# A block of attention, state space scan and routed LoRA on one core: the router's small steps split between VectorE and GpSimd, and the order of all queues written anew

## What is computed

```python
h = layernorm(x) * (1 + ca) + sa
xn = ln(h)
attn_out = causal_attention(xn, 16 heads of 16) @ o_w + o_b
x_c = silu(causal_conv4(xn @ in_proj_w[:, :512]) + conv_b);  z = xn @ in_proj_w[:, 512:]
dt = softplus(x_dbc[..., :16] @ dt_w + dt_b);  B, C = x_dbc[..., 16:32], x_dbc[..., 32:48]   # x_dbc = x_c @ x_proj_w
for t: state = exp(dt * A) * state + (x_c * dt) * B;  y[t] = sum_n C * state     # 512 channels, 16 states each
r = h + alpha * attn_out + (1 - alpha) * (((y + x_c * D) * silu(z)) @ ssm_out_w)
r = r + gelu(ln(r) @ ffn_w1 + b1) @ ffn_w2 + b2
x = x + ga * r
g = layernorm(x) * (1 + cb) + sb
logits = g @ router_w + router_b                    # 8 experts
w = softmax(where(logits < second_largest, -1e9, logits))
x = x + gb * (g @ base_w + base_b + 2.0 * sum_e w[e] * (g @ A_e) @ B_e)
```

## Time and profile before

| | us |
|---|---|
| median of 3 runs | 5759.91 (5759.66 to 5764.49) |
| the profiled execution, its own time | 5763.4 |
| its span from first to last instruction | 5761.6 |
| one turn of the loop (the softplus sum starts at 108.6 and, 31 turns on, at 5479.2) | 173.25 |

### The profile page before, as it was taken

The page is one execution under the profiler, slowest core; times in us unless marked ns, Lnnn a source line. Parts: engine busy times, 40 slices in busy tenths (PEclk is TensorE's granted clock), DMA queues, the critical chain, the costliest instruction groups (busy, mean ns, idle before and its releaser), DMA issues.

```text
span 5761.6 us, 94560 instructions
## 1 busy us (share of the span) xinstructions
PE 5214.0 (90%) x32280; PEld 3490.0 (61%) x32280; DVE 5161.4 (90%) x7776; ACT 4082.5 (71%) x6407; POOL 4217.8 (73%) x2545
## 2 busy tenths in 40 slices
PE   4799998999999999999999999999999999999986
PEld 2466665666666566666566656666656666666664
DVE  4999999999999999999999999999999999999983
ACT  3777777767777777777777777777777777777763
POOL 3777777777777777777777777777777777777762
PEclk7899999999999999999999999999999999999998
DMA  4444445444444444444444445444454445554441
GB/s 127 145 146 140 146 143 147 146 148 133 151 136 153 143 145 140 145 142 154 142 143 138 142 150 151 143 138 143 143 155 147 142 139 146 143 151 145 140 128 39
DMA packets 521455, 812.22 MB, mean 141 GB/s; under 512 B 80432, under 2 KB 227288, under 8 KB 520976
## 3 DMA queue, kind: packets, MB, share of 16 engines
q1 hardware_dynamic: 513072, 805.79, 46.5%
q10 hardware_dynamic: 7904, 0.39, 0.1%
HBM read 716.50 MB, written 88.38 MB: 140 GB/s over the span
## 4 chain that ended last, share of the span: by engine, by line
PE 54%; DVE 22%; ACT 10%; issue 9%; DMA 1%; POOL 1%; SPq 1%; DVEq 0%; POOLq 0%; ACTq 0%
PE pY L931 8%; PE pM L1073 8%; PE pM L1082 7%; DVE pD L1192 6%; PE pM L953 4%; DVE state L1200 4%; PE pM L1062 4%; PE pM L1006 4%; DVE mx L1250 3%; PE pM L1037 3%; DVE xc L1232 3%; PE pM L1019 2%; PE pM L940 2%; PE pM L988 2%; DVE state L1192 2%
## 5 line engine op out<-in xcount | busy, mean ns | idle before, releaser
L575 POOL TENSOR_TENSOR state<-scan_in,bc 128x1024 f32<-128x1024 f32 x1024 | 2426.1, 2382 | 852.7 <-PE pY L931 603.1
L1192 DVE TENSOR_TENSOR_SCAN pD<-pD,state 128x512 f32<-128x512 f32 x1536 | 1830.0, 1215 | 111.9 <-ACT pD L699 96.8
L699 ACT ACTIVATE pD<-scan_in,A 128x512 f32<-128x512 f32 x2048 | 1391.7, 686 | 432.8 <-DVE state L1200 336.0
L931 PE MATMUL pY<-ident,state 128*128 128x128 f32 x8192 | 1180.7, 280 | 13.0 <-DVE state L1200 8.5
L931 PEld LDWEIGHTS pY<-ident,state 128*128 128x128 f32 x8192 | 934.9, 145 | 258.8 <-issue 178.3
L1200 DVE TENSOR_TENSOR state<-pD,bc 128x512 f32<-128x512 f32 x1536 | 1030.6, 682 | 23.6 <-DMA bc<-bc_d 8.7
L800 ACT ACTIVATE region<-pM 128x512 f32<-128x512 f32 (+1 forms) x1408 | 754.1, 555 | 329.6 <-PE pM L1039 303.9
L1250 DVE TENSOR_REDUCE mx<-pM 128x1 f32<-128x512 f32 (+3 forms) x1408 | 857.1, 628 | 122.0 <-PE pM L1021 119.5
L1037 PE MATMUL pM<-region 98*128 98x512 bf16 (+3 forms) x2048 | 559.8, 318 | 269.2 <-ACT region L800 149.8
L562 POOL TENSOR_TENSOR state<-state,bc 128x512 f32<-128x512 f32 x512 | 647.5, 1273 | 205.0 <-DVE state L1192 175.5
L1019 PE MATMUL pM<-region 96*128 96x512 bf16 (+3 forms) x2048 | 548.2, 305 | 92.9 <-DVE mx L1250 71.6
...
## 6 DMA issues: line engine op xcount, KB each, us to landing
bc<-bc_d SPq DMA_DIRECT2D x2048, 256.0 KB, 4.1
...
region<-qk_d SPq DMA_DIRECT2D x256, 64.0 KB, 3.1
...
```

What stands on the lines that cost most here:

```text
L575: nc.gpsimd.tensor_tensor(state[:, at_:at_ + JP], us[:, parity(b), k // N * JP:(k // N + 1) * JP, :], bc[:, k % BC_SLOTS, 0, :].unsqueeze( ...
L699: act.activation(pD[DECAY_BANK[e]][:], dts[:, parity(b), j], ACT.Exp, scale=A[:, j, n:n + 1]).then_inc(a_ok.sem, 1)
L931: ins = pe.matmul(y_part(t, e % JP), state[:, e % RING, t * P:(t + 1) * P], ident[:], is_transpose=True, start=False, stop=(e % PASS >= PA ...
L1192: v.tensor_tensor_scan(h if e in POOL_C else decay, decay, h, 0.0, ALU.mult, ALU.add)\
```

## The change

1. `sp3` becomes `sp3_0` and `sp3_1`, two instructions over 128x1024; `dt_ok` and `u_ok` are counted by halves. `u0` waits for the first half, `u1` for the second, `fill0` for `u0`, `fill16` for `u1`, `dec0` for the first and `dec32` for the second half.
2. `fillK` raises `b_ok` by 1 instead of 2, and `scanE` waits for unit E//2.
3. The router. `keep` is made by four `tensor_scalar` instructions of 128x8, with the second largest as a scalar from memory. The subtraction moves to POOL (step `route`) and writes a new tensor `lgs`; `route2` waits for it and for `keep`. The product with `keep` moves to POOL (`wkeep`). Sum and reciprocal stay on DVE in a step of their own (`esum`). The last product moves to POOL (`wnorm`); its factor 2.0 is folded into `w_lb` in the setup, one more instruction there. `lora` on DVE is then only the last multiply.
4. Waits: `mxG_0` on DVE loses its wait for PE's turning of the maxima two groups back; in `oeG` and `fillK` the same waits stand in another order.
5. New lists for all five queues and new banks. The lists hold the same steps but for those named above, at other places.

```diff
                 e, at_ = k * JP, k * JP % RING
-                if k == 0:
-                    b.wait(pool, u_ok)
-                b.wait(pool, *row_in(b, k, 0))
-
                 if e >= RING:
                     b.wait(pool, y_ok, e + JP - RING)
                 else:
                     b.wait_last(pool, y_ok, SCANS + e + JP - RING)
+                if k % N == 0:
+                    b.wait(pool, u_ok, k // N + 1)
+                b.wait(pool, *row_in(b, k, 0))
                 nc.gpsimd.tensor_tensor(state[:, at_:at_ + JP], us[:, parity(b), k // N * JP:(k // N + 1) * JP, :],
                                         bc[:, k % BC_SLOTS, 0, :].unsqueeze(1).broadcast_to([P, JP, L]),
-                                        ALU.mult).then_inc(b_ok.sem, JP)
+                                        ALU.mult).then_inc(b_ok.sem, 1)
 ...
                     half = slice(int(name[1]) * J // 2, (int(name[1]) + 1) * J // 2)
-                    b.wait(pool, dt_ok)
+                    b.wait(pool, dt_ok, int(name[1]) + 1)
                     nc.gpsimd.tensor_tensor(us[:, par, half], dts[:, par, half], xc[:, half], ALU.mult)\
                       .then_inc(u_ok.sem, 1)
 ...
+                elif name == "route":
+
+                    b.wait(pool, rt_c)
+                    nc.gpsimd.tensor_tensor(lgs[:], lg[:], top[:, :, 0:1].broadcast_to([P, TB, E]), ALU.subtract)\
+                      .then_inc(rk_ok.sem, 1)
+                elif name == "wkeep":
+
+                    b.wait(pool, ex_ok)
+                    b.wait(pool, kp_ok)
+                    nc.gpsimd.tensor_tensor(ew[:], ew[:], keep[:], ALU.mult).then_inc(wk_ok.sem, 1)
+                elif name == "wnorm":
+
+                    b.wait(pool, es_ok)
+                    nc.gpsimd.tensor_tensor(ew[:], ew[:], esum[:].unsqueeze(2).broadcast_to([P, TB, E]), ALU.mult)\
+                      .then_inc(ew_ok.sem, 1)
 ...
-                if e == 0:
-                    b.wait(act, dt_ok)
+                if e % PASS == 0:
+                    b.wait(act, dt_ok, e // PASS + 1)

 ...
                 elif name == "route2":
-                    b.wait(act, rt_c)
-                    act.activation(ew[:], lg[:], ACT.Exp).then_inc(ex_ok.sem, 1)
+                    b.wait(act, rk_ok)
+                    b.wait(act, kp_ok)
+                    act.activation(ew[:], lgs[:], ACT.Exp).then_inc(ex_ok.sem, 1)
 ...
+            link(v.tensor_scalar(w_lb[:], w_lb[:], LORA_SCALE, None, ALU.mult))
 ...
-                b.wait(dve, b_ok, e + 1)
                 b.wait(dve, a_ok, e + 1)
+                b.wait(dve, b_ok, e // JP + 1)
 ...
-                elif name == "sp3":
-                    par = parity(b)
+                elif name in ("sp3_0", "sp3_1"):
+                    par, half = parity(b), slice(int(name[4]) * JP, (int(name[4]) + 1) * JP)
                     b.wait(dve, dt_e)
-                    v.tensor_tensor(dts[:, par], dts[:, par], us[:, par], ALU.add).then_inc(dt_ok.sem, 1)
+                    v.tensor_tensor(dts[:, par, half], dts[:, par, half], us[:, par, half], ALU.add)\
+                     .then_inc(dt_ok.sem, 1)
                 elif name[:2] == "mx":
                     g, e = int(name[2]), int(name[4:])
-                    if e == 0:
-                        if g >= 2:
-                            b.wait(dve, s_ps, 12 * (g - 1))
-                        else:
-                            b.wait_last(dve, s_ps, 12 * (g + 3))
 ...
                     b.wait(dve, rt_c, 5)
-                    v.tensor_tensor(keep[:], lg[:], top[:, :, 1:2].broadcast_to([P, TB, E]), ALU.is_ge)\
-                     .then_inc(rt_c.sem, 1)
-                    b.wait(dve, rt_c, 6)
-                    v.tensor_tensor(lg[:], lg[:], top[:, :, 0:1].broadcast_to([P, TB, E]), ALU.subtract)\
-                     .then_inc(rt_c.sem, 1)
+                    for t in range(TB):
+                        v.tensor_scalar(keep[:, t, :], lg[:, t, :], top[:, t, 1:2], None, ALU.is_ge).then_inc(kp_ok.sem, 1)
+                elif name == "esum":
+                    b.wait(dve, wk_ok)
+                    v.tensor_reduce(esum[:], ew[:], AX_X, ALU.add).then_inc(es_ok.sem, 1)
+                    b.wait(dve, es_ok, 1)
+                    v.reciprocal(esum[:], esum[:]).then_inc(es_ok.sem, 1)
                 elif name == "lora":
-                    b.wait(dve, ex_ok)
-                    v.tensor_tensor(ew[:], ew[:], keep[:], ALU.mult).then_inc(ew_ok.sem, 1)
-                    b.wait(dve, ew_ok, 1)
-                    v.tensor_reduce(esum[:], ew[:], AX_X, ALU.add).then_inc(ew_ok.sem, 1)
-                    b.wait(dve, ew_ok, 2)
-                    v.reciprocal(esum[:], esum[:]).then_inc(ew_ok.sem, 1)
-                    b.wait(dve, ew_ok, 3)
-                    v.scalar_tensor_tensor(out=ew[:], in0=ew[:], scalar=LORA_SCALE,
-                                           in1=esum[:].unsqueeze(2).broadcast_to([P, TB, E]),
-                                           op0=ALU.mult, op1=ALU.mult).then_inc(ew_ok.sem, 1)
                     b.wait(dve, la_ps)
                     b.wait(dve, ew_ok)
```

Of the new lists, the stretches of which the prediction speaks (the diff rewrites all lines; `...` where steps are left out):

```diff
     "POOL": """
-        ... -x2 -x2b fill14 -l3s +ql0 fill15 +ql1 pc30 fill16 fill17 +ql2 fill18 -xb pc31 fill19 -gb -put fill20 ...
+        ... pc23 -x2 -x2b fill14 -l3s +ql0 fill15 fill16 pc30 -xb +ql1 -route -wkeep fill17 -wnorm pc31 +ql2 ...
-        ... fill29 pc54 pc55 fill30 fill31 +u0 +u1 +fill0 pc62 pc63 +fill1 ...
+        ... fill29 pc54 pc55 fill30 fill31 +u0 +fill0 +u1 pc62 pc63 +fill1 ...
     "ACT": """
-        ... +qk1 dec30 st0_1_2 +qm1 +qk2 -h3t0 -h3t1 +xs1 dec31 +qm2 dec32 -route2 st0_1_3 st0_2_0 dec33 ...
+        ... +qk1 dec30 +qm1 dec31 -h3t0 +xs1 -h3t1 dec32 +qk2 dec33 -route2 st0_1_2 st0_1_3 dec34 ...
-        ... mt3 dec55 st2_3_0 dec56 +dt3 dec57 oe2 dec58 +sp2 st3_0_0 dec59 ...
+        ... dec57 +dt3 oe2 st3_1_0 dec58 dec59 +sp2 dec60 st3_1_1 ...
     "PE": """
-        ... st3_3_0 add60 pv3_1 +z0 pv3_2 pv3_3 +v0 on3 add61 add62 add63 +v1 ot0 ot1 yt0 +skip0 yt1 +add0 yt2 +mx0_2
-        yt3 +add1 +add2 sso0 +add3 sso1 +mx0_3 +z1 +add4 +add5 +add6 +mx0_4 +z2 +mx0_5 ... h2t0 h2t1 ...
+        ... +v0 add57 +mx0_3 st3_1_2 st3_1_3 add58 pv3_0 st3_2_0 st3_2_2 pv3_1 st3_3_0 pv3_2 add59 pv3_3 +z0 +v1 on3
+        add60 add61 +mx0_4 add62 add63 ot0 ot1 +skip0 yt0 yt1 yt2 +add0 yt3 +add1 +add2 sso0 sso1 +add3 +z1 ...
     "DVE": """
-        ... -f2_1 scan26 c26 mx1_1 scan27 c27 mx1_2 +qk0 -l3s scan28 mx1_3 c28 +xs0 +qk1 scan29 scan30 +qk2 c29 +xs1
-        -route scan31 -lora scan32 scan33 mx1_4 c32 ...
+        ... -f2_1 mx1_2 mx1_3 scan27 mx1_4 mx1_5 c27 mx1_6 +qk0 -l3s mx1_7 mx1_8 scan28 scan29 +xs0 c28 +qk1 c29 scan30
+        scan31 +xs1 scan32 -route mx1_9 mx1_10 c32 +qk2 -esum scan33 -lora mt1 scan34 ...
-        ... +mx0_0 on2 c57 +mx0_1 +sp3 c58 scan59 c59 scan60 c60 scan61 c61 scan62 scan63 +scan0 +c0 on3 gate1 +scan1
+        ... +mx0_0 on2 +mx0_1 scan59 +mx0_2 c58 +sp3_0 +mx0_3 c59 scan60 c60 scan61 +sp3_1 c61 scan62 scan63 +scan0
+        +scan1 on3 gate1 +c0 +c1 +mx0_4 +scan2 +c2 +scan3 ...
```

123 lines of the change are left out of this document (62 added, 61 removed).

## The result

The changed kernel takes 5538.2 us (median of 4 runs, 5536.2 to 5541.9), the kernel before 5759.8 beside it: a ratio of 0.962 (95% interval 0.961 to 0.963). That is 222 us less, where 110 were forecast and 195 were the end of the range. The direction was right, the size half of what came. The profiled execution took 5536.2 us, its span 5534.4. A turn is 166.0 us now ((5263.02 - 115.65) / 31, from the starts of `sp3_0`), 7.2 less; the forecast was 3.55 less.

The account below looks back on a forecast made before the run. It took a loop of a DVE leg and a PE leg as the bound: new legs 109.1 + 58.1 = 167.2, plus 2.5 waits, 169.7 us a turn, 3.55 less; times 31 turns 110 less, 5650 us, range 5565 to 5745.

Parts of the forecast that it names:

- The two-leg reading: A turn is DVE's work from `f2_1` to `c60`, 101.4 us, then PE's from `add60` to `f2_1`, 71.9.
- the first leg: DVE's stretch from `f2_1`, ending at `c60` before and `c2` after; forecast 109.1 us in the new lists, plus 2.5 of waits.
- the list sum: Step prices added along the old loop gave 101.0 + 68.5 us, 3.7 short of the trace, put down to waits and clock.
- rival B: Router alone gains, lists nothing, as some loop through ACT or POOL is as long; 96 us less, 5664; 18%.
- The waits that I added, 2.5: New waits a turn on top of 167.2 us: 0.6 for `keep`, 1.0 for the softplus halves, 0.9 for PE's tighter leg.
- `keep` 0.6: Wait of the router's four `keep` instructions on DVE for POOL: 0.6 us a turn, half a `ql1`.
- The halves 1.0: Waits of `sp3_0` and `sp3_1` on DVE for POOL's fills, 1.0 us a turn for both; their head start gains nothing.
- The 0.9 for density: PE has 13.8 us more beside the DVE leg; DVE waits for `mx` or PE for `st` banks, 0.9 us a turn.
- C: Shared DVE/POOL pair, mild form: the first `keep` instruction waits a whole fill, 2.36 us for 0.6; 5705; 12%.
- E: Slower, shared pair in strong form: `keep` waits 4.8 us for `pc30`, `xb`, `ql1`, each softplus half a fill; 5867; 12%.
- D: PE's idle time in the DVE leg can't be squeezed; turn 173.3 us, no change, 5760; 8%.
- A: The loop in full with no new waits: 6.05 us a turn, 188 less, 5572; 12%.

Follow-up runs that it names:

- b_pad_early: The kernel before with row maximum `mx1_9` done two times more on DVE into a spare tile, about 1.3 us a turn; 5803.0 us against 5763.6.
- b_no_ln: The kernel before with the softplus logarithm replaced by a second exponential, so two table loads go (dt wrong); 5685.2 us against 5760.4.
- a_no_ln: The changed kernel with the softplus logarithm replaced by a second exponential, so two table loads go (dt wrong); 5533.1 us, ratio 0.961.
- a_old_router: The changed kernel's lists, halves and counts, with the router's old steps on DVE and POOL's three router steps taken out; 5671.7 us, ratio 0.984.
- b_new_router: The kernel before, in its old lists, with the router as in the change; 5781.1 us, ratio 1.003.
- b_one_input: The kernel before with `keep` and the subtraction each as four one-input instructions on DVE; 5830.4 us, ratio 1.012.
- b_drained: The old lists with the new router, POOL's list arranged to have run empty when `keep` comes; 5739.1 us against 5760.4 for the kernel before.
- b_cut: The kernel before without the router's mask (`keep`, subtraction, product with `keep`), output not the reference's; 5716.5 us against 5768.8.

## Why the prediction was right or wrong

- **The two-leg reading**: right that what is added to DVE in the first leg is paid (b_pad_early), wrong that DVE sets this leg alone, and wrong about where the chain runs. It does not stay on DVE for some 100 us: in the turn shown it leaves DVE for PE at 2651.72, after 49. The page said it: the chain of before is 54% PE and 22% DVE, where legs of 101.4 and 71.9 us would give DVE 58%. I read the chain's direction and not its shares.
- **The step that failed** is how the list sum was brought to the trace. The prices of the old loop were 3.7 us short of it, 3.4 of them in PE's leg (68.5 against 71.9). I named waits and clock as the reason and then carried all of it into the new legs: 71.9 - 13.8 = 58.1. The leg was 55.6. The prices alone give 68.5 - 13.8 = 54.7, 0.9 short. Most of the 3.4 was not in the leg's own work: the window began at the end of `c60`, and PE came to `add60` 2.1 us after it, late after the waits of 1.74 us for DVE and 1.72 for ACT's softplus, and at a clock of 0.67. The lists took this away; b_no_ln and a_no_ln show how much the softplus held up, 75 us in the old lists and 5 in the new. What the other 1.3 are was not found, and some of them stayed. Of the 3.65 us a turn by which the forecast fell short, 2.5 are this leg (58.1 against 55.6); 1.4 are waits in the other (111.6 against 110.2); the turn shown is 0.2 shorter than the mean. "Some loop through ACT or POOL, which I did not add up" stood in rival B, as a reason for a smaller gain; it was there, and its removal made the gain larger.
- **The waits that I added, 2.5**: in the turn shown the first leg is 110.2, so 1.1 over the sum. `keep` 0.6: measured 0.1 (245 ns against 217, four times). The halves 1.0: the mean of 1581 ns against a least of 1224 gives 0.7. The 0.9 for density: 0.3 is left for it.
- **In parts**: forecast for the router 3.1 - 0.6 = 2.5 a turn, measured 4.3 in the new lists. 0.5 is the wait that did not come; 0.4 is `keep`, which takes 2.03 us in the new lists and not 1.59 when left in its old form; 1.2 is PE's clock behind the stall, which I had nowhere. These are 2.1 where 1.8 are to be explained; the subtraction, 1.19 us and not 1.36 in those lists, takes 0.2 off. Forecast for the rest 2.95 - 1.9 = 1.05, measured 3.0. Of this the halves are worth 1.5, which I had at nothing.
- **Place, not form**: the count of POOL's queue against DVE's was right to 0.2 us, and `keep` met none of `pc30`, `xb` and `ql1`. But the count alone would not have saved it: in a_old_router the same place lets `fill17` catch `keep`. That C and E did not come about is also the work of POOL's step `route`, which the change put ahead of `fill17`, and the prediction didn't see this guard. The mechanism behind them is real all the same: b_new_router and b_one_input are C at another place. I had taken LayerNorm's statistics beside a running POOL instruction as the lower bound; for TENSOR_SCALAR it doesn't hold.
- **Covered work**: `esum` and `lora` wait 2.4 us in the whole run, as said. POOL's small operations are covered. PE is idle 6.7 us in the first leg, below the 8 that I had named as the limit, so D fell.
- **Signs that were wrong**: PE's busy time was to stay and fell by 97 us (clock). ACT's wait ahead of `route2` was to stay at 3 us and went, since POOL is free when the maxima are there. The scans' wait for fills did rise, from 11.0 to 36.2 us, which I had called a sign of failure; it is 0.8 us a turn and was outweighed.
- **The rivals**: A, the full loop without waits, 5572, was the nearest, and 34 us too high: it too carried over the difference of PE's leg (2.5 a turn), and leaving out all waits (1.1) hid a part of that. B failed as a whole: in the old lists the router alone gives 21 us (b_drained) or costs 18 (b_new_router), not 96.
- **What stays open**: in the old lists DVE's busy time fell by 76 us in b_cut and by 79 in b_drained, and the time by 47 and 21. In b_cut the chain goes mostly over PE; which step of PE's list ties it was not found, nor why `lora` one scan later costs 22 us.
